# One recurrence with two-set corrections, in-place transposes and a loop in two parts

## The chip, the cores and the metric

The kernel runs on one core of a Trainium2 chip. The metric is the device time of one execution in microseconds (us); smaller is better. TensorE is called PE (its weight loads PEld), VectorE DVE, ScalarE ACT, GpSimd POOL and SyncE SP.

## What is computed

Two residual blocks act on x of 4 x 256 x 32 x 32 floats. The first is a test-time-training layer: after a group norm and a layer norm, 1024 tokens of each image are projected to queries, keys and values of 8 heads of width 32, and a recurrence runs over chunks of 16 tokens. The second is a convolution-like block on a 5 x 5 self-correlation. Only the recurrence is touched:

```
def step(carry, inp):                       # 64 chunks, one after the other
    W1c, b1c = carry
    xq, xk, xv, et = inp
    Z1 = xk @ W1c + b1c
    grad = _ln_l2_bwd(Z1, xv - xk, g, bb)   # gradient of a layer norm's L2 loss
    Attn1 = jnp.tril(xq @ xk.swapaxes(-1, -2))
    b1_bar = b1c - jnp.tril(et) @ grad
    Z1_bar = xq @ W1c - et * Attn1 @ grad + b1_bar
    last_eta = et[..., -1, :, None]
    W1n = W1c - (last_eta * xk).swapaxes(-1, -2) @ grad
    b1n = b1c - (last_eta * grad).sum(-2, keepdims=True)
    return ((W1n, b1n), xq + _ln(Z1_bar, g, bb, EPS_IN))
```

## The kernel before

The recurrence is 64 chunks (`NC`), each for 4 images x 8 heads at once: 128 partitions are 4 pairs of heads x 32 rows (2 heads x 16 tokens), and the free dimension is 4 images x 32. Each engine has an instruction stream written out by hand, and the order between engines comes from counted semaphores, one increment per chunk. ACT, DVE and POOL have all 64 chunks written out; PE writes out chunks 0, 1, 62 and 63 and runs chunks 2 to 61 in a loop of 15 trips of four chunks (`run_chunks`, L1114). A wait whose count depends on the loop variable is computed in registers at the head of a trip.

The trick that shapes the order is that Z of the next chunk is not computed from the updated state. PE forms a *base* for chunk c+1 from the state before the gradient of chunk c is in it (`base`, L1136 to L1160; its last matmul, L1158, adds the bias), and then, when that gradient is known, adds a *correction* to the same PSUM bank (`grads(ZW, ZB[p], o, 1)`, L1167: 16 matmuls of 32x32, which stand as 32 in the trace because every fp32 matmul is two). The correction needs `AM`, the masked key and query products of the chunk.

One chunk c, engine by engine, in program order:

- **PE** (`body`, L1197): waits for the gradient GL of chunk c-1 (`gl`), its masks (`am`) and for the copied products of chunk c (`s1`); correction; `update` of the state with KHX and GL (L1179) and of the bias (L1187); the attention correction of the outputs (L1167 again); a `filler` that computes nothing used (L1194); base of chunk c+1, which waits for the key blocks KT2 from POOL (`kt2`), the query copy (`qr`) and the copied state (`wcopy`); query base (L1231).
- **ACT** (`body`, L1556 on): square of Z after the correction; `out_store` (L1548) of the output rows of chunk c-5; square of output rows (L1538); square root of the variance (L1562) and the variance (L1565), which wait for a DVE sum; `state_w` (L1497), the copy of the updated state that base waits for; `state_b` (L1501); in chunks 40 to 47 a piece of the following stage's scaling (`gain`, L803); `khx` (L1508), `qt2` (L1524), `next_k` (L1517), `products` (L1531, waits for base); square root for the outputs (L1544).
- **DVE** (`body`, L1298 on): sums and the centred Z (L1300 to L1305); target (L1308); reciprocal (L1314); Y (L1319); Y times centred Z (L1322); its two sums (L1323, L1325); two small coefficients (L1328, L1332); YC (L1336), WX (L1338) and GL = WX + YC (L1341); then for older chunks the output variance (`out_var`, L1284), a 32x32 block transpose of output rows (`out_turn`, L1294) and the copy of output rows out of PSUM (`out_rows`, L1279).
- **POOL** (`body`, L1421 on): two small products (L1423, L1426) after DVE's reciprocal; YL (L1428); `blocks` (KT2 of chunk c+2, L1395); `masks` (AM of chunk c+1, L1411, waits for products); `out_norm` of chunk c-3 (L1419, waits for the transpose of chunk c-4, which DVE runs after GL of chunk c); `queries` of chunk c+2 (L1403). In chunk 56 `pre` (L1449) of the following stage comes ahead of `blocks`.

SP only issues DMAs paced by `gl`; none is on the path of a chunk.

## Time and profile before

| what | us |
|---|---|
| median of 3 runs | 583.49 (583.01 to 584.29) |
| the profiled execution | 581.06 |
| its span, first to last instruction | 579.2 |
| first and last `products` of the recurrence start at | 166.8 and 445.9 |
| busy: PE, DVE, ACT, POOL | 483.9, 432.1, 346.2, 327.8 |

All times in the rows are us from the start of the span; durations of single instructions in the lists are in us. A row of the timeline gives the start, the time until the instruction ended, the engine, the source line, operation, operands, how many instructions are merged (x32), and in brackets the idle time before with what ended it. "issue" means that nothing in the profile held the engine back. Instructions of DVE, ACT and POOL overlap a little: the next one starts before the one ahead has written its last result.

### The profile page before, as it was taken

What the parts mean: (1) busy time and instruction counts of PE and PEld (TensorE: products, weight loads), DVE (VectorE), ACT (ScalarE), POOL (GpSimd) and SP (SyncE); (2) the same over time, 40 slices, a digit from 0 to 9 for tenths busy, and PEclk for the clock granted to TensorE, in tenths of its full rate; (3) what the DMA queues carried; (4) which work ended last, traced back from release to release, by engine and by line L of the source; (5) the groups of instructions that cost most, each with busy time, mean ns of one, the idle gap of its engine ahead of it and who ended that gap; (6) DMA issues with size and microseconds to landing.
All of it is one profiled execution on the core that took longest, in us unless ns stands there. A gap on an engine that the chain in (4) does not pass through costs nothing.

```text
span 579.2 us, 30352 instructions
## 1 busy us (share of the span) xinstructions
PE 483.9 (84%) x12556; PEld 313.8 (54%) x12556; DVE 432.1 (75%) x1526; ACT 346.2 (60%) x1166; POOL 327.8 (57%) x590
## 2 busy tenths in 40 slices
PE   0699889898558789888888888888887699998996
PEld 0344334443346577777777676666675244456563
DVE  4757788888746789888888888888885667676652
ACT  2344334322246788888888889988885487553321
POOL 1276888787734466666666655565763667330112
PEclk9999989899858999999999999999997899998998
DMA  8310111111101011111111000011010500000123
GB/s 338 123 24 14 37 37 36 38 36 36 39 9 32 22 37 28 33 32 33 33 28 37 1 1 1 19 36 37 19 37 4 171 1 2 1 2 1 74 75 145
DMA packets 15136, 24.74 MB, mean 43 GB/s; under 512 B 4228, under 2 KB 4968, under 8 KB 15080
## 3 DMA queue, kind: packets, MB, share of 16 engines
q1 hardware_dynamic: 15080, 24.10, 13.8%
q8 instruction: 23, 0.38, 0.3%
q14 instruction: 33, 0.27, 0.2%
HBM read 11.50 MB, written 4.19 MB: 27 GB/s over the span
## 4 chain that ended last, share of the span: by engine, by line
PE 25%; DVE 24%; ACT 12%; issue 8%; POOL 2%; POOLq 0%; ACTq 0%
PE PS L1167 6%; PE PS L924 4%; PE PS L1255 3%; PE PS L906 3%; ACT work L1556 3%; PE PS L361 2%; DVE work L1341 2%; DVE work L1336 2%; DVE work L1322 2%; DVE work L1300 2%; DVE work L1319 2%; DVE PS L1338 2%; DVE PS L1323 2%; DVE PS L1302 2%; DVE PS L1325 2%
## 5 line engine op out<-in xcount | busy, mean ns | idle before, releaser
L1167 PE MATMUL PS<-work 32*32 32x32 f32 x4064 | 59.6, 194 | 37.9 <-DVE work L1341 21.0
L1167 PEld LDWEIGHTS PS<-work 32*32 32x32 f32 x4064 | 53.8, 108 | 43.4 <-issue 43.1
L1411 POOL TENSOR_TENSOR work<-work,mask 128x256 f32<-128x256 f32 x64 | 46.8, 731 | 35.7 <-ACT work L1531 35.7
L512 PE MATMUL PS<-X,work 128*128 128x512 f32 x128 | 63.2, 641 | 0.3 <-ACT X L435 0.3
L1423 POOL TENSOR_TENSOR work<-work,lrh 128x4 f32<-128x4 f32 x64 | 12.9, 201 | 75.6 <-DVE work L1314 70.1
L1300 DVE TENSOR_REDUCE work<-work 128x4 f32<-128x128 f32 x64 | 18.3, 286 | 49.2 <-ACT work L1556 49.2
L663 POOL TENSOR_TENSOR work<-work 128x512 f32<-128x512 f32 x32 | 43.8, 1370 | 7.1 <-DVE work L582 7.1
L1152 PEld LDWEIGHTS PS<-work 64*32 64x32 f32 x2048 | 32.9, 110 | 24.9 <-issue 23.6
L1152 PE MATMUL PS<-work 64*32 64x64 f32 x2048 | 43.6, 225 | 2.9 <-issue 2.0
L1194 PE MATMUL PS<-cst 128*128 128x256 f32 x126 | 45.1, 440 | 0.0
L1179 PE MATMUL PS<-work 32*64 32x32 f32 x2016 | 43.0, 222 | 2.2 <-issue 2.2
L1508 ACT ACTIVATE work<-TK,small 128x128 f32<-128x128 f32 x128 | 44.3, 402 | 0.0
L1524 ACT ACTIVATE work<-QP,cst 128x128 f32<-128x128 f32 x128 | 43.9, 396 | 0.0
L1395 POOL TENSOR_TENSOR work<-KP,cst 128x256 f32<-128x256 f32 x64 | 39.2, 612 | 6.5 <-POOLq L454 6.5
L512 PEld LDWEIGHTS PS<-X,work 128*128 128x128 f32 x128 | 25.3, 206 | 29.5 <-issue 28.7
L881 POOL TENSOR_TENSOR TK<-TK 128x512 f32<-128x512 f32 x7 | 9.0, 1304 | 53.5 <-ACT TK L1077 53.5
L1179 PEld LDWEIGHTS PS<-work 32*64 32x64 f32 x2016 | 35.8, 135 | 3.9 <-issue 1.3
L581 DVE TENSOR_TENSOR work<-PS,work 128x512 f32<-128x512 f32 x32 | 21.8, 683 | 21.4 <-POOL KP L666 19.1
L1544 ACT ACTIVATE work<-work,small 128x4 f32<-128x4 f32 x64 | 19.0, 296 | 24.7 <-DVE work L1284 24.6
L377 ACT ACTIVATE work<-X 128x512 f32<-128x512 f32 (+1 forms) x16 | 9.7, 630 | 40.0 <-DVE X L368 40.0
L1255 PE MATMUL PS<-TK,wsm 128*128 128x512 f32 x64 | 31.4, 616 | 1.5 <-ACT X L1600 1.5
L1158 PE MATMUL PS<-work,cst 128*128 128x128 f32 x128 | 32.2, 334 | 0.0
(162 smaller groups left out, 1344.5 us busy)
## 6 DMA issues: line engine op xcount, KB each, us to landing
X<-in_x SPq DMA_DIRECT2D x4, 1024.0 KB, 8.2
TK<-KP SPq DMA_DIRECT2D x64, 64.0 KB, 1.9
X<-QP SPq DMA_DIRECT2D x64, 64.0 KB, 2.0
TK<-in_x SPq DMA_DIRECT2D x16, 256.0 KB, 3.0
out<-TK SPq DMA_DIRECT2D x16, 256.0 KB, 2.4
work<-in_rope SPq DMA_DIRECT2D x2, 512.0 KB, 9.1
cst<-in_consts SPq DMA_DIRECT2D x1, 289.0 KB, 5.0
work<-in_wk SPq DMA_DIRECT2D x1, 256.0 KB, 11.2
```

The lines of the kernel that those rows point to most:

```text
L512: mm = nc.tensor.matmul(PS[:, 2 + m, :], lhs(j), xt(i, j), start=(j == 0), stop=(j == J - 1))
L663: nc.gpsimd.tensor_tensor(ksw[:, t, :], ksw[:, t, :], sinT[:, h], ALU.mult).then_inc(s_ksin, 1)
L1152: mm = nc.tensor.matmul(PS[HD * a:HD * a + HD, ZB[p], b * ZW:b * ZW + ZW], KT2[p][r:r + 64, k * B + b, :, :].rearrange("p e t -> p (e t)") ...
L1158: nc.tensor.matmul(PS[:, ZB[p], 0:B * ZW].rearrange("p (b n) -> p b n", b=B)[:, :, 0:HD], ident, Bs[1 - p if past(n, 1) else 0], start=Fal ...
L1167: mm = nc.tensor.matmul(PS[HD * a:HD * a + HD, bank, b * width:b * width + HD], AM[p][HD * a:HD * a + HD, b, part, :, :].rearrange("p e t ...
L1179: mm = nc.tensor.matmul(PS[2 * HD * a2:2 * HD * a2 + 2 * HD, WB + k, b * HD:b * HD + HD], KHX[p][HD * a:HD * a + HD, b, :, :].rearrange("p ...
L1194: nc.tensor.matmul(PS[:, QB[p], 256:512], ident, ccol("spread", 0, 256), start=True, stop=True, skip_group_check=True)
L1255: mm = nc.tensor.matmul(PS[:, 2 + m, :], wsm[:, j, m * P:(m + 1) * P], ot(i, j), start=(j == 0), stop=(j == J - 1))
L1395: nc.gpsimd.tensor_tensor(KT2[p], chunk(KP, c).unsqueeze(2).broadcast_to([P, J * B, E, CS]), ccol("emask_k").unsqueeze(1).unsqueeze(3).bro ...
L1411: nc.gpsimd.tensor_tensor(AM[p].rearrange("p b s e t -> p (b s) e t"), S1[p].unsqueeze(2).broadcast_to([P, 2 * B, E, CS]), mask2.rearrange ...
L1508: kx = nc.scalar.activation(KHX[p][:, :, e, :].rearrange("p b (f t) -> p b f t", f=E), head_rows(1, c), ACT.Copy, scale=upd_mask[:, e:e + 1])
L1524: a = nc.scalar.activation(QT2[p][:, :, e, :], chunk(QP, c), ACT.Copy, scale=ccol("emask_k", e, 1))
```

## The change

PE adds the correction in two sets: one from YC as soon as that exists, one from WX, and the second releases ACT; GL is awaited afterwards, for the update. The filler stays in chunks 1 to 13 and is gone after; the PE loop becomes two loops, of 3 trips with filler and 12 without, and the query base becomes a function. DVE reorders its sums and coefficients, runs `out_var` ahead of GL, and transposes output rows straight into `TT`, so ACT's `out_store` and the buffer ZT go. ACT runs `products` before `qt2`. POOL runs `out_norm` and `queries` first, then waits for GL of its own chunk, then `masks` and `blocks`. WX moves from PSUM to SBUF.

```diff
-        TS, SQ, YL, YC = (carve(B, HD) for _ in range(4))
+        TS, SQ, YL, YC, WX = (carve(B, HD) for _ in range(5))
         YY = carve(2, B, HD)
...
             def run_chunks(eng, body):
                 for c in range(2):
-                    body(c, c % 2)
-                with nc.Fori(0, NC // 4 - 1, engines=(mybir.EngineType.PE,), hint_back_edge=True) as four:
-                    for k in range(4):
-                        body(four * 4 + (2 + k), k % 2)
+                    body(c, c % 2, fill=True)
+                for first, trips, fill in ((2, FILLED, True), (2 + 4 * FILLED, NC // 4 - 1 - FILLED, False)):
+                    with nc.Fori(0, trips, engines=(mybir.EngineType.PE,), hint_back_edge=True) as four:
+                        for k in range(4):
+                            body(four * 4 + (first + k), k % 2, fill=fill)
                 for c in range(NC - 2, NC):
                     body(c, c % 2)
+            FILLED = 3
...
-                def grads(width, bank, p, part):
+                def grads(width, bank, p, part, rows):
...
-                def body(c, p):
-                    o = 1 - p
-                    done, now, nxt = value(pe, c), value(pe, c + 1), value(pe, c + 2)
-                    before = value(pe, c - 1) if past(c, 2) else None
-                    if past(c, 1):
-                        pe.wait_ge(q["init"], 1)
-                        pe.wait_ge(q["gl"], done)
-                        pe.wait_ge(q["am"], done)
-                        pe.wait_ge(q["s1"], now)
-                        grads(ZW, ZB[p], o, 1).then_inc(q["corr"], 1)
-                        pe.wait_ge(q["init"], 1)
-                        pe.wait_ge(q["khx"], done)
-                        pe.wait_ge(q["bcopy"], done)
-                        update(o)
-                        grads(HD, QB[o], o, 0).then_inc(q["attn"], 1)
-                        if past(c, 2):
-                            pe.wait_ge(q["zq"], before)
-                        filler(p)
-                    else:
-                        base(0, 0, 1, 1)
-                    if not is_last(c):
-                        base(c + 1, o, nxt, now)
-                    else:
-                        pe_mean(pe, 0, True)
+                def query_base(ready, p, drained):
                     pe.wait_ge(q["init"], 1)
-                    pe.wait_ge(q["qt2"], now)
-                    pe.wait_ge(q["wcopy"], now)
-                    if past(c, 2):
-                        pe.wait_ge(q["zq"], before)
+                    pe.wait_ge(q["qt2"], ready)
+                    pe.wait_ge(q["wcopy"], ready)
+                    if drained is not None:
+                        pe.wait_ge(q["zq"], drained)
...
                     mm.then_inc(q["qbase"], 1)
+                def body(c, p, fill=False):
+                    o = 1 - p
+                    done, now, nxt = value(pe, c), value(pe, c + 1), value(pe, c + 2)
+                    before = value(pe, c - 1) if past(c, 2) else None
+                    if past(c, 1):
+                        pe.wait_ge(q["init"], 1)
+                        pe.wait_ge(q["yc"], done)
+                        pe.wait_ge(q["am"], done)
+                        pe.wait_ge(q["s1"], now)
+                        grads(ZW, ZB[p], o, 1, YC)
+                        pe.wait_ge(q["init"], 1)
+                        pe.wait_ge(q["w"], done)
+                        grads(ZW, ZB[p], o, 1, WX).then_inc(q["corr"], 1)
+                        pe.wait_ge(q["init"], 1)
+                        pe.wait_ge(q["gl"], done)
+                        pe.wait_ge(q["khx"], done)
+                        pe.wait_ge(q["bcopy"], done)
+                        update(o)
+                        grads(HD, QB[o], o, 0, GL[o]).then_inc(q["attn"], 1)
+                        if fill:
+                            if before is not None:
+                                pe.wait_ge(q["zq"], before)
+                            filler(p)
+                    else:
+                        base(0, 0, 1, 1)
+                    if not is_last(c):
+                        base(c + 1, o, nxt, now)
+                    else:
+                        pe_mean(pe, 0, True)
+                    query_base(now, p, before)
...
                     dve.wait_ge(q["zn"], c + 1)
-                    nc.vector.transpose(ZT.rearrange("p b d -> p (b d)"), ZN.rearrange("p b d -> p (b d)")
-                                        ).then_inc(q["zt"], 1)
+                    nc.vector.transpose(
+                        TT.rearrange("p e (b n) -> p b e n", b=B)[:, :, :, c * CS:(c + 1) * CS],
+                        ZN.rearrange("p b (e t) -> p b e t", e=E)).then_inc(q["ot"], 1)
...
                     nc.vector.tensor_tensor(YY[:, 0, :, :], PZ, TS, ALU.add).then_inc(q["y"], 1)
                     dve.wait_ge(q["y"], c + 1)
                     dve.wait_ge(q["zc"], c + 1)
+                    nc.vector.tensor_reduce(sums[:, 0:B], YY[:, 0, :, :], AX.X, ALU.add).then_inc(q["my"], 1)
                     nc.vector.tensor_tensor(YY[:, 1, :, :], YY[:, 0, :, :], ZC, ALU.mult).then_inc(q["yp"], 1)
-                    nc.vector.tensor_reduce(sums[:, 0:B], YY[:, 0, :, :], AX.X, ALU.add).then_inc(q["my"], 1)
-                    dve.wait_ge(q["yp"], c + 1)
-                    nc.vector.tensor_reduce(sums[:, B:2 * B], YY[:, 1, :, :], AX.X, ALU.add).then_inc(q["m"], 1)
                     dve.wait_ge(q["u"], c + 1)
                     dve.wait_ge(q["my"], c + 1)
                     nc.vector.scalar_tensor_tensor(cc0, sums[:, 0:B], -1.0 / HD, lead[:, 0, :],
                                                    ALU.mult, ALU.mult).then_inc(q["cy"], 1)
+                    dve.wait_ge(q["yp"], c + 1)
+                    nc.vector.tensor_reduce(sums[:, B:2 * B], YY[:, 1, :, :], AX.X, ALU.add).then_inc(q["m"], 1)
+                    dve.wait_ge(q["yl"], c + 1)
+                    dve.wait_ge(q["cy"], c + 1)
+                    nc.vector.tensor_tensor(YC, YL, bc(cc0), ALU.add).then_inc(q["yc"], 1)
                     dve.wait_ge(q["m"], c + 1)
                     dve.wait_ge(q["u2"], c + 1)
                     nc.vector.scalar_tensor_tensor(cc1, sums[:, B:2 * B], -1.0 / HD, lead[:, 1, :],
                                                    ALU.mult, ALU.mult).then_inc(q["c"], 1)
-                    dve.wait_ge(q["yl"], c + 1)
-                    dve.wait_ge(q["cy"], c + 1)
-                    nc.vector.tensor_tensor(YC, YL, bc(cc0), ALU.add).then_inc(q["yc"], 1)
                     dve.wait_ge(q["c"], c + 1)
                     nc.vector.tensor_tensor(WX, ZC, bc(cc1), ALU.mult).then_inc(q["w"], 1)
-                    dve.wait_ge(q["w"], c + 1)
                     dve.wait_ge(q["yc"], c + 1)
-                    nc.vector.tensor_tensor(GL[p], WX, YC, ALU.add).then_inc(q["gl"], 1)
                     if past(c, 2):
                         out_var(c - 2)
+                    dve.wait_ge(q["w"], c + 1)
+                    nc.vector.tensor_tensor(GL[p], WX, YC, ALU.add).then_inc(q["gl"], 1)
...
                     if past(c, 1):
-                        pool.wait_ge(q["zt"], c + 0)
+                        pool.wait_ge(q["ot"], c + 0)
                     nc.gpsimd.tensor_tensor(ZN, ZQ[c % 3], bc(sdq[1 - p]), ALU.mult).then_inc(q["zn"], 1)
...
-                    if not near_end(c):
-                        blocks(c + 2, p)
-                    if not is_last(c):
-                        masks(c + 1, 1 - p)
                     if past(c, 3):
                         out_norm(c - 3, 1 - p)
                     if not near_end(c):
                         queries(c + 2, p)
+                    pool.wait_ge(q["gl"], c + 1)
+                    if not is_last(c):
+                        masks(c + 1, 1 - p)
+                    if not near_end(c):
+                        blocks(c + 2, p)
...
-                def out_store(c):
-                    act.wait_ge(q["zt"], c + 1)
-                    nc.scalar.activation(
-                        TT.rearrange("p e (b n) -> p e b n", b=B)[:, :, :, ds(c * CS, CS)],
-                        ZT.rearrange("p b (e t) -> p e b t", e=E), ACT.Copy).then_inc(q["ot"], 1)
...
-                    if not is_last(c):
-                        qt2(c + 1, 1 - p)
                     if not isinstance(c, int) or c + 3 < NC:
                         next_k(c + 2, p)
                     if not is_last(c):
                         products(c + 1, 1 - p)
+                        qt2(c + 1, 1 - p)
```

## Rows read from the trace of the kernel before

**Rows 1.** Busy times by stretch: start and end, length, busy us and instructions, PEclk, DMA.

```profile
178.00:198.00 20.00, 15.59 (x688) 12.12 (x688) 14.21 (x70) 13.84 (x57) 9.63 (x27) 1.00 0.10 23
...
248.20:264.90 16.70, 14.82 (x688) 11.82 (x688) 14.65 (x73) 14.05 (x60) 10.57 (x29) 1.00 0.13 32
```

**Rows 2.** Timeline of ACT in one chunk.

```profile
303.61 0.28 ACT L1556 ACTIVATE work<-PS 128x128 f32<-128x128 f32 x1
...
304.63 0.42 ACT L1497 ACTIVATE work<-PS 128x128 f32<-128x128 f32 x2
...
306.47 0.36 ACT L1531 ACTIVATE work<-PS,small 128x128 f32<-128x128 f32 x1
...
307.68 0.28 ACT L1556 ACTIVATE work<-PS 128x128 f32<-128x128 f32 x1
```

**Rows 3.** Timeline of DVE in the same chunk.

```profile
305.03 0.29 DVE L1319 TENSOR_TENSOR work<-PS,work 128x128 f32<-128x128 f32 x1
305.36 0.29 DVE L1322 TENSOR_TENSOR work<-work,PS 128x128 f32<-128x128 f32 x1
...
306.76 0.29 DVE L1341 TENSOR_TENSOR work<-PS,work 128x128 f32<-128x128 f32 x1
307.01 0.29 DVE L1284 TENSOR_REDUCE work<-work 128x4 f32<-128x128 f32 x1
307.21 0.30 DVE L1294 STREAM_TRANSPOSE work<-work 128x128 f32<-128x128 f32 x1
```

**Rows 4.** Timeline of PE in the same chunk.

```profile
304.71 0.70 PE L1194 MATMUL PS<-cst 128*128 128x256 f32 x2
305.34 0.65 PE L1152 MATMUL PS<-work 64*32 64x64 f32 x32
...
307.16 0.45 PE L1167 MATMUL PS<-work 32*32 32x32 f32 x32 [0.36 <-DVE work L1341]
307.54 0.67 PE L1179 MATMUL PS<-work 32*64 32x32 f32 x32
```

**Rows 5.** Timeline of the one chunk in which POOL is late (57).

```profile
416.33 0.62 POOL L1395 TENSOR_TENSOR work<-KP,cst 128x256 f32<-128x256 f32 x1
...
416.90 0.78 POOL L1411 TENSOR_TENSOR work<-work,mask 128x256 f32<-128x256 f32 x1
...
417.64 0.39 POOL L1419 TENSOR_TENSOR work<-work 128x128 f32<-128x128 f32 x1
...
417.99 0.28 POOL L1403 COPY work<-QP 128x128 f32<-128x128 f32 x1
...
418.45 0.52 PEld L1152 LDWEIGHTS PS<-work 64*32 64x32 f32 x32 [1.49 <-issue]
```

**Rows 6.** Timeline of ACT in a chunk with a piece of the scaling.

```profile
348.44 0.69 ACT L1524 ACTIVATE work<-QP,cst 128x128 f32<-128x128 f32 x2
349.02 0.30 ACT L1517 ACTIVATE work<-KP 128x128 f32<-128x128 f32 x1
```

**Rows 7.** Timeline of PE in the loop's first trip, one of its stalls.

```profile
183.86 0.67 PE L1179 MATMUL PS<-work 32*64 32x32 f32 x32 [1.18 <-issue]
```

**Rows 8.** DMA queues that fetch instructions, from 172 to 198.

```profile
q8 instruction: 6, 0.10, 1.5%
```

**Rows 9.** DMA queues from 198.5 to 437, all that moved anything.

```profile
q1 hardware_dynamic: 3891, 5.84, 9.4%
q14 instruction: 24, 0.20, 0.3%
```

**Rows 10.** Timeline of PE after the loop ends, chunk 62.

```profile
440.55 0.44 PE L1167 MATMUL PS<-work 32*32 32x32 f32 x17 [3.11 <-issue]
440.93 1.08 PE L1179 MATMUL PS<-work 32*64 32x32 f32 x32
...
446.83 0.67 PE L1179 MATMUL PS<-work 32*64 32x32 f32 x32
```

**Rows 11.** Busy times by stretch, as rows 1, in that chunk.

```profile
441.00:443.00 2.00, 2.00 (x73) 1.83 (x73) 1.59 (x8) 1.80 (x9) 0.28 (x2) 0.50 0.03 8
```

More of the change, by code:

```diff
@@ L760, in build @@
         ZQ = [carve(B, HD) for _ in range(3)]
-        SQQ, ZN, ZT = (carve(B, HD) for _ in range(3))
+        SQQ, ZN = (carve(B, HD) for _ in range(2))
         ss, sz, ssq, sd1 = (carve(B) for _ in range(4))
@@ L776, in home @@
             return PS[:, 7, at * B * HD:(at + 1) * B * HD].rearrange("p (b d) -> p b d", b=B)
-        PZ, WX, ZC = (home(at) for at in range(3))
-        at = 3 * B * HD
+        PZ, ZC = (home(at) for at in range(2))
+        at = 2 * B * HD
         cc0, sums = PS[:, 7, at:at + B], PS[:, 7, at + B:at + 3 * B]
@@ L1098, in build @@
             names = ("init my cy updw wcopy bcopy kt2 qt2 qr kr khx base qbase corr s1 am p sq ss sz zc v sd r ts y yp m u u2 "
-                     "yl c w yc gl upd attn zq sqq ssq sdq rq zn zt ot").split()
+                     "yl c w yc gl upd attn zq sqq ssq sdq rq zn ot").split()
             q = {n: sem(f"scan_{n}") for n in names}
@@ L1169, in grads @@
                                                       "p e t -> p (e t)"),
-                                                  GL[p][HD * a:HD * a + HD, b, :],
+                                                  rows[HD * a:HD * a + HD, b, :],
                                                   start=False, stop=True, skip_group_check=True)
@@ L1233, in body @@
                                     QT2[p][r:r + 64, k * B + b, :, :].rearrange("p e t -> p (e t)"),
-                                    R[o][r:r + 64, k, b, 0:HD], start=(b == 0), stop=False,
+                                    R[1 - p][r:r + 64, k, b, 0:HD], start=(b == 0), stop=False,
                                     skip_group_check=True)
                     mm.then_inc(q["qbase"], 1)
+                def body(c, p, fill=False):
[28 more added lines that the diff above has]
+                    query_base(now, p, before)
                 run_chunks(pe, body)
@@ L1240, in _ @@
                 pe.wait_ge(q["am"], NC)
-                grads(HD, QB[1], 1, 0).then_inc(q["attn"], 1)
+                grads(HD, QB[1], 1, 0, GL[1]).then_inc(q["attn"], 1)
                 def project(i, first):
@@ L1354, in _ @@
                 out_var(NC - 2)
-                dve.wait_ge(q["ot"], NC - 4)
                 out_turn(NC - 4)
@@ L1361, in _ @@
                 out_r(NC - 1)
-                dve.wait_ge(q["ot"], NC - 3)
                 out_turn(NC - 3)
@@ L1365, in _ @@
                 dve_scale(dve, 0)
-                dve.wait_ge(q["ot"], NC - 2)
                 out_turn(NC - 2)
-                dve.wait_ge(q["ot"], NC - 1)
                 out_turn(NC - 1)
@@ L1556, in body @@
                     nc.scalar.activation(SQ, zb, ACT.Square).then_inc(q["sq"], 1)
-                    if past(c, 5):
-                        out_store(c - 5)
                     if past(c, 2):
@@ L1615, in _ @@
                 out_square(NC - 2, 0)
-                out_store(NC - 5)
                 out_sd(NC - 2, 0)
-                out_store(NC - 4)
                 out_square(NC - 1, 1)
@@ L1622, in _ @@
                 out_sd(NC - 1, 1)
-                out_store(NC - 3)
                 act_square(act, 1, False)
                 act_affine(act, 0)
-                out_store(NC - 2)
-                out_store(NC - 1)
                 act.wait_ge(q["ot"], NC)
```

## Prediction

> **What bounds the kernel now.** I looked first for the stretch that repeats. Of the recurrence's 64 chunks, 60 are 15 trips of one PE loop, so a change in a chunk counts sixty-fold. The busy times by stretch show the loop's first trip, 688 matmuls in 20.0 us, and a later trip, the same 688 in 16.70 us at a granted clock of 1.00, the upper of its two levels (2.4 GHz) [rows 1]. No engine is full: in those 16.70 us PE is busy for 14.82, DVE 14.65, ACT 14.05, POOL 10.57. A chain through all of them sets the time. The timeline of one chunk shows it: ACT's square at 303.61 begins the chunk, the next square comes at 307.68, so a chunk is 4.07 [rows 2]; four make 16.28, and the head of a trip, where waits are computed in registers, adds the other 0.42. I count from the square. DVE's sums run on to GL, which starts at 3.15 and ends at 3.44 [rows 3]; PE's correction starts 0.11 later, at 3.55, and the next square 0.52 after that [rows 4, 2]. So the chain today is square, DVE, GL, correction, and GL's 0.33 is what the change goes for. Second comes a chain that nearly keeps up: the state copy ends at 1.44, the filler holds base until 1.73, products start at 2.86 and end at 3.22 [rows 2, 4]. The correction needs the products too, and here they wait 0.3 for GL.
>
> **DVE's new order.** A step that needs the one ahead starts 0.33 after it, one that does not 0.20 [rows 3]. From Y at 1.42: its sum at 1.75, the product at 1.95, the small coefficient at 2.15, the second sum at 2.28, YC at 2.47 (YL permitting), the other coefficient at 2.67, WX at 2.87, the old output variance at 3.07, GL at 3.27. WX ends at 3.16, so the input of the last correction is 0.28 sooner than GL was, and GL itself is 0.12 later. WX in SBUF instead of PSUM I cost at nothing: GL writes SBUF today in the same 0.29.
>
> **PE's two sets.** A set of 32 takes 0.38 to issue [rows 4]. The first set also has the waits on the products in front of it, though it is released by YC. This is the first thing that turns against the change: products must now be there 0.38 earlier. Without filler, base can start at 1.44 + 0.11 (that step from one engine to PE was seen above). Base to products is 1.13 [rows 4, 2] (there ACT came free at the same moment, so it is an upper end), products take 0.36, then 0.11 to PE, 0.38 for the first set and 0.52 from the second set to the square. The chunk is 1.55 + 2.50 = 4.05, the same as today. The removed output store on ACT does not shorten it, since it stood where ACT waits for DVE's first sum; moving `qt2` behind the products only takes it out of a place where it now ends just in time. With the filler (0.63 [rows 4]) base starts at 1.73 and the chunk is 4.23.
>
> **POOL's new order.** The output normalisation waits for a transpose that DVE runs after GL. Before, nothing urgent stood behind it; now `queries`, `masks` and `blocks` do, and PE's base waits for `blocks`. After GL at 3.27 the transpose starts 0.25 later and takes 0.30 [rows 3], 0.11 to POOL (as above, an estimate), then one after the other 0.35, 0.28, 0.74 and 0.62, read from the one chunk in which POOL ran without a pause; there PE's base started 0.18 after POOL's last needed instruction [rows 5]. KT2 of chunk c+2 is thus usable 3.27 + 0.25 + 0.30 + 0.11 + 1.99 + 0.18 = 6.10 after the square of chunk c, and the square of chunk c+2 comes 2.50 after that. Two chunks take 8.60, one 4.30. This is above both 4.05 and 4.23, so I take it for filled and unfilled chunks alike. POOL is then free again at 5.92 - 4.30 = 1.62, about when DVE's reciprocal, the step ahead of Y at 1.42, lets it start the next chunk, so YL is late by a tenth at most. The masks have a chunk to spare. A trip is 2 x 8.60 + 0.42 = 17.62 against 16.70, 0.92 more. If POOL's spans flatter me and it is off the path, a trip is 4 x 4.05 + 0.42 = 16.62 (-0.1); if the transpose takes twice its 0.30 because it writes runs of 16, a chunk is 4.45 and a trip 18.2 (+1.5). I take 0.92 because each link is a row of the same instructions.
>
> **What that adds up to.** Trips at the steady rate: the second and third of the first loop, and of the second loop's twelve all but the first and the two with the pieces of scaling: 11 x 0.92 = +10.1 (bounds -1.1 and +16.5). In the eight chunks with scaling ACT's products end the wait; `qt2` ahead of them took 0.58 [rows 6], the earlier need takes 0.38 back, 8 x 0.20 = -1.6, of which I count -1.2 because the heads of two trips are no longer hidden there.
>
> **Code loading.** The first trip took 20.0 for the matmuls of a 16.7 trip: PE stops for issue, once for 1.18 [rows 7], and q8, a queue that carries instructions, moves six packets then and none in the later trips, while q14 goes on throughout [rows 8, 9]. That is 29.1 ns for each matmul with its weight load [rows 1]. A trip grows from 688 matmuls to 816 with filler and 808 without. First loop, first trip: 816 x 29.1 = 23.7, +3.7 on the 20.0 of before. Second loop, first trip: 23.5 where the old loop ran on in 16.7, +6.8. The lower bound of that is the old first trip, +3.3; the upper adds the stall of 3.11 with which PE left its loop [rows 10], +9.9. Chunks 62 and 63 I leave as they are: one set more and no filler.
>
> Sum: 10.1 - 1.2 + 3.7 + 6.8 = +19.4 on the profiled execution's 581.06, so 600.5. The median of the runs is 2.4 above that execution; 603 is the forecast for the median.
>
> **Rivals.** *The first loop does not stay loaded.* Today q8 is silent between 198.5 and 437 [rows 9], so 688 matmuls with their loads stay. 816 is a fifth more. If they do not, its two later trips cost 23.7 instead of 17.62, +12: 615. The Trainium skill (Runtime: NRT & Kernel Launch, Instruction fetch mechanics) gives PE room for 2048 instructions, by which an estimated 1670 (two for each matmul, and the waits) would fit. It also says that a taken branch to outside a window of two blocks fetches anew. For the loop of before the trace agrees with the first and not with the second [rows 9]. This rival has 8%.
>
> *The clock stays down.* After the 3.11 stall PE ran at 0.50, the lower level (1.2 GHz), and the chunk from one update to the next took 5.90 [rows 10, 11] before the clock came back, with filler in it. The change from loop to loop brings such a stall, and behind it is no filler. PE's own 3.71 a chunk (14.82 over four) becomes 3.46; scaled by 5.90/3.71 it is 5.5, 1.2 over 4.30, for 44 chunks +53: 656. Against it: the stalls of the first trip, up to 1.18 [rows 7], left the clock at 1.00 [rows 1]. The Trainium skill (TensorE: Matmul & The Clock Gate, Part 1) has the slow level as the default and activity as what lifts it, a rule that speaks against taking filler away; no row here shows a recovery without filler. This rival has 8%.
>
> *The gradient chain alone sets the chunk*, the other side. If products end by 2.78 and `blocks` a quarter of a microsecond sooner than I say, the chunk is WX's 3.16 + 0.11 + 0.52 = 3.79, a trip 15.58, 11 x -1.12 = -12.3; with -1.2 and the code's +10.5 that is -3.0, 580.5. It decides at the wait for the products: base would have to start 0.3 ahead of the state copy that it waits for. I give it 5%.
>
> *A draw* needs POOL off the path and the second loop's code nearly free: -1.1 - 1.2 + 3.7 and next to nothing for its entry. I give it 3%.
>
> **How the numbers follow.** The main case has 76%. Its own bounds go from 603 - 10.1 - 1.1 - 3.5 = 588 (POOL off the path, cheap entry) to 603 + 6.4 + 3.1 = 612; the first rival at 615 with a little more for a slower transpose makes 618. Outside are the clock (8%), the other side (5%), a draw (3%) and the tails. Within 0.2% (1.2 us, about what a measurement of this kernel can tell from no change) I call the same. Slower has everything but the last two rivals: 92%.
>
> **What would show it.** Right: the first set waits for ACT's products, not for DVE's YC; the normalisation on POOL starts just after DVE's transpose, and base waits for `blocks`, not for ACT; squares 4.2 to 4.4 apart with and without filler; a first trip of 23 to 24 us in both loops, with instruction packets at the second one's start. Wrong: squares 3.8 apart, or the second loop entered without a stall; or a PE clock of 0.50 beyond the second loop's first trip.

## The result and the profile after

The changed kernel takes 620.71 us (median of 4 runs, 618.82 to 624.09) against 583.89 (583.01 to 586.09): ratio 1.0631, 95% interval 1.0576 to 1.0686. The profiled execution took 620.45, its span is 618.6 us and its mean granted clock 0.873; before, 581.06, 579.2 and 0.959. Ratios here leave disturbed runs out while medians take in every run, so that for one kernel below, the one without filler, the two don't match.

The page of the changed kernel, costliest groups (last part: idle time ahead of the group and what ended it), answers first who waits for whom.

```profile
L1170 PE MATMUL PS<-work 32*32 32x32 f32 x6080 | 88.8, 207 | 26.6 <-ACT work L1541 14.2
...
L1427 POOL TENSOR_TENSOR work<-work 128x128 f32<-128x128 f32 x64 | 25.6, 400 | 92.9 <-DVE TK L1305 89.8
L1155 PE MATMUL PS<-work 64*32 64x64 f32 x2048 | 51.3, 250 | 23.1 <-POOL work L1403 16.5
```

The same two PE groups in the kernel before:

```profile
L1167 PE MATMUL PS<-work 32*32 32x32 f32 x4064 | 59.6, 194 | 37.9 <-DVE work L1341 21.0 <-ACT work L1531 7.7 <-POOL work L1411 5.9
L1152 PE MATMUL PS<-work 64*32 64x64 f32 x2048 | 43.6, 225 | 2.9 <-issue 2.0 <-ACT work L1497 1.0
```

PE's correction sets (L1170) now wait for ACT's products (L1541), and for DVE in two places only (2.4 us, was 21.0). Of the 14.2 us put down to the products, 8.6 stand at the heads of 11 trips, where the products had ended 0.5 to 0.8 earlier and the time is the head's own work in registers (experiment 6); the other 5.7, in 30 places, are a wait for them. POOL's output normalisation (L1427) waits 89.8 us for DVE's transpose, and base (L1155) waits 16.5 for POOL's blocks (L1403). One chunk of the first loop, in which PE still has its filler, shows the same links in a timeline (start, us, engine and line).

```profile
213.55 0.28 ACT L1560 ACTIVATE work<-PS 128x128 f32<-128x128 f32 x1 [0.17 <-PE PS L1170]
...
214.52 0.61 POOL L1403 TENSOR_TENSOR work<-KP,cst 128x256 f32<-128x256 f32 x1
...
214.65 0.63 DVE L1320 TENSOR_TENSOR work<-TK,work 128x128 f32<-128x128 f32 x1
...
215.34 0.65 PE L1155 MATMUL PS<-work 64*32 64x64 f32 x32
...
216.36 0.28 DVE L1344 TENSOR_TENSOR work<-work,PS 128x128 f32<-128x128 f32 x1
...
216.45 0.37 ACT L1541 ACTIVATE work<-PS,small 128x128 f32<-128x128 f32 x1 [0.51 <-PE PS L1161]
...
216.74 0.29 DVE L1350 TENSOR_TENSOR work<-PS,work 128x128 f32<-128x128 f32 x1
...
216.96 0.74 PE L1170 MATMUL PS<-work 32*32 32x32 f32 x64 [0.17 <-ACT work L1541]
217.15 0.28 DVE L1355 TENSOR_TENSOR work<-work 128x128 f32<-128x128 f32 x1
...
217.34 0.30 DVE L1305 STREAM_TRANSPOSE TK<-work 128x128 f32<-128x128 f32 x1
...
217.73 0.40 POOL L1427 TENSOR_TENSOR work<-work 128x128 f32<-128x128 f32 x1 [1.42 <-DVE TK L1305]
217.75 0.28 ACT L1560 ACTIVATE work<-PS 128x128 f32<-128x128 f32 x1 [0.17 <-PE PS L1170]
...
218.85 0.35 DVE L1320 TENSOR_TENSOR work<-TK,work 128x128 f32<-128x128 f32 x1
...
219.01 0.66 POOL L1403 TENSOR_TENSOR work<-KP,cst 128x256 f32<-128x256 f32 x1
...
219.77 0.65 PE L1155 MATMUL PS<-work 64*32 64x64 f32 x32 [0.17 <-POOL work L1403]
```

The square comes at 213.55 and again at 217.75, 4.20 later. YC (L1344) is done at 216.64, the products (L1541) at 216.82, and both sets (64 matmuls) start at 216.96: the first set's early input buys nothing. WX (L1350), the second set's input, is done at 217.03, before that set's turn: a set takes 0.38 to issue [rows 4]. POOL's normalisation starts 0.09 after the transpose ends, and 2.04 later base starts.

The windows (length; busy us and instructions of PE, PEld, DVE, ACT, POOL; granted clock; DMA) tell the rest. They are the first loop's first trip and, roughly, its third; the second loop's first; a later one; and a stretch of low clock.

```profile
178.40:203.00 24.60, 20.70 (x820) 16.54 (x824) 13.82 (x70) 13.54 (x56) 10.30 (x27) 0.78 0.11 26
...
222.80:240.50 17.70, 16.36 (x824) 13.24 (x825) 14.89 (x72) 13.44 (x56) 10.46 (x29) 1.00 0.12 30
...
240.50:267.50 27.00, 21.63 (x816) 18.12 (x816) 14.21 (x72) 13.96 (x57) 11.94 (x30) 0.61 0.12 29
...
278.00:295.40 17.40, 13.85 (x814) 11.93 (x812) 14.41 (x72) 13.50 (x57) 9.81 (x28) 1.00 0.11 28
...
359.99:376.10 16.11, 16.11 (x611) 13.97 (x614) 10.66 (x54) 11.19 (x43) 8.24 (x23) 0.50 0.00 1
```

A trip at the upper clock is 17.70 with filler, where it was 16.70 [rows 1]. Without filler the window shown has 17.40, but it begins two chunks behind a low stretch; the one trip whose four chunks (30 to 33) all ran at the upper clock took 17.73. In the second loop the clock doesn't stay up. From 359.99 on, PE is busy all of 16.11 us and does only three chunks' matmuls, at 0.50, the lower level (1.2 GHz). A chunk that is low from end to end takes 5.37 to 5.40. The matmuls around the place where it fell are these:

```profile
338.98 0.65 PE L1155 MATMUL PS<-work 64*32 64x64 f32 x32 [0.90 <-POOL work L1403]
341.26 0.74 PE L1170 MATMUL PS<-work 32*32 32x32 f32 x64 [0.82 <-ACT work L1541]
...
355.28 0.47 PE L1170 MATMUL PS<-work 32*32 32x32 f32 x32
356.64 0.65 PE L1155 MATMUL PS<-work 64*32 64x64 f32 x32 [0.90 <-POOL work L1403]
...
358.86 1.08 PE L1170 MATMUL PS<-work 32*32 32x32 f32 x64 [0.77 <-ACT work L1541]
359.87 1.08 PE L1182 MATMUL PS<-work 32*64 32x32 f32 x32
```

Behind two ordinary waits at the head of a trip, 0.90 and 0.77, the 32 update matmuls take 1.08 instead of 0.67. There is no long stall, and one trip earlier the like waits, 0.90 and 0.82, were followed by no fall. Later the clock comes back by itself and falls again. Of chunks 18 to 61, 13 ran low in whole or in part (leaving out a tenth of chunk 25, and chunk 61, in which PE leaves the loop).

Where the time went, from square to square (us):

| chunks | before | after | difference | forecast |
|---|---|---|---|---|
| 0 to 2, with the start of 0 | 178.69 | 178.36 | -0.3 | 0 |
| 2 to 6, first loop's first trip | 20.58 | 24.67 | +4.1 | +3.7 |
| 6 to 14, its other trips | 33.47 | 37.51 | +4.0 | +1.8 |
| 14 to 18, second loop's first trip | 16.67 | 26.94 | +10.3 | +6.8 |
| 18 to 41 and 49 to 62, the rest of that loop | 155.50 | 174.45 | +18.9 | +8.3 |
| 41 to 49, scaling but for its first chunk | 36.16 | 35.12 | -1.0 | -1.2 |
| 62, 63 and all after it | 138.15 | 141.60 | +3.5 | 0 |

The differences add up to the +39.4 between the two profiled executions. Scaling lengthens chunks 40 to 47; chunk 40, which ran low, stands in the row above. The 13 low chunks took 71.2 us; the same 13 at the length of their neighbours at the upper clock would be an estimated 57.9. So about 13.3 of the 18.9 in chunks 18 to 41 and 49 to 62 is the clock, and 5.6 is what else is longer.

### The profile page after: what moved, and what is told of

It reads as the page before. It is cut to its first block, busy times and chain, and to the rows that moved or that the text cites. A ratio compares the mean times of both kernels' runs of the same rounds, so it can differ in the third digit from the quotient of the medians.

```text
span 618.6 us, 34244 instructions
## 1 busy us (share of the span) xinstructions
PE 514.3 (83%) x14472; PEld 351.3 (57%) x14472; DVE 430.0 (70%) x1526; ACT 338.6 (55%) x1102; POOL 330.1 (53%) x590
## 3 DMA queue, kind: packets, MB, share of 16 engines
HBM read 11.50 MB, written 4.19 MB: 25 GB/s over the span
## 4 chain that ended last, share of the span: by engine, by line
PE 42%; issue 11%; POOL 8%; ACT 6%; DVE 6%; POOLq 0%; ACTq 0%; DVEq 0%
PE PS L1170 9%; PE PS L1155 6%; PE PS L1161 4%; PE PS L1182 4%; PE PS L924 3%; PE PS L1266 3%; PE PS L361 3%; PE PS L906 3%; PE PS L1190 2%; PE PS L1210 2%; POOL work L1419 2%; POOL work L1403 2%; ACT work L1541 2%; PE PS L946 1%; PE PS L1197 1%
## 5 line engine op out<-in xcount | busy, mean ns | idle before, releaser
L1170 PE MATMUL PS<-work 32*32 32x32 f32 x6080 | 88.8, 207 | 26.6 <-ACT work L1541 14.2
L1170 PEld LDWEIGHTS PS<-work 32*32 32x32 f32 x6080 | 82.9, 120 | 33.2 <-issue 31.2
L1427 POOL TENSOR_TENSOR work<-work 128x128 f32<-128x128 f32 x64 | 25.6, 400 | 92.9 <-DVE TK L1305 89.8
L1155 PE MATMUL PS<-work 64*32 64x64 f32 x2048 | 51.3, 250 | 23.1 <-POOL work L1403 16.5
L1155 PEld LDWEIGHTS PS<-work 64*32 64x32 f32 x2048 | 40.1, 126 | 32.9 <-issue 30.8
L1182 PE MATMUL PS<-work 32*64 32x32 f32 x2016 | 49.9, 239 | 2.5 <-issue 2.3
L1541 ACT ACTIVATE work<-PS,small 128x128 f32<-128x128 f32 x64 | 23.5, 367 | 51.7 <-PE PS L1161 51.7
L1182 PEld LDWEIGHTS PS<-work 32*64 32x64 f32 x2016 | 43.3, 155 | 6.6 <-issue 2.8
L1403 POOL TENSOR_TENSOR work<-KP,cst 128x256 f32<-128x256 f32 x64 | 40.8, 637 | 5.3 <-POOLq L454 5.3
L1560 ACT ACTIVATE work<-PS 128x128 f32<-128x128 f32 x64 | 17.8, 278 | 33.3 <-PE PS L1170 32.6
L1210 PE MATMUL PS<-work 64*32 64x32 f32 x2048 | 33.5, 210 | 0.0
```

Of the source, the lines that this page charges most:

```text
L1155: mm = nc.tensor.matmul(PS[HD * a:HD * a + HD, ZB[p], b * ZW:b * ZW + ZW], KT2[p][r:r + 64, k * B + b, :, :].rearrange("p e t -> p (e t)") ...
L1170: mm = nc.tensor.matmul(PS[HD * a:HD * a + HD, bank, b * width:b * width + HD], AM[p][HD * a:HD * a + HD, b, part, :, :].rearrange("p e t ...
L1182: mm = nc.tensor.matmul(PS[2 * HD * a2:2 * HD * a2 + 2 * HD, WB + k, b * HD:b * HD + HD], KHX[p][HD * a:HD * a + HD, b, :, :].rearrange("p ...
L1210: mm = nc.tensor.matmul(PS[HD * a:HD * a + HD, QB[p], b * HD:b * HD + HD], QT2[p][r:r + 64, k * B + b, :, :].rearrange("p e t -> p (e t)") ...
L1403: nc.gpsimd.tensor_tensor(KT2[p], chunk(KP, c).unsqueeze(2).broadcast_to([P, J * B, E, CS]), ccol("emask_k").unsqueeze(1).unsqueeze(3).bro ...
L1541: nc.scalar.activation(S1[p].rearrange("p (b s) t -> p b (s t)", b=B), PS[:, ZB[p], 0:B * ZW].rearrange("p (b n) -> p b n", b=B)[:, :, HD:ZW],
```

## The experiments

The first theory: taking the filler out of the second loop lets the clock fall, entering a second loop costs its code, and the longer trip comes from products and POOL. The rival is that chunks are long because of the order of the work alone, and the clock only follows.

**1. One loop, all filled.** The changed kernel with a single loop of 15 trips, so that neither a second loop nor an unfilled chunk up to 61 is left.

```diff
-for first, trips, fill in ((2, FILLED, True), (2 + 4 * FILLED, NC // 4 - 1 - FILLED, False)):
+for first, trips, fill in ((2, NC // 4 - 1, True),):
```

> The changed kernel with one loop of 15 trips, filler in every chunk. If taking the filler away is what lets the clock fall: granted clock 1.00 from chunk 2 to 61, trips of about 17.5 us as in chunks 6 to 13 of the changed kernel, no code fetched in mid-loop, 597 to 601 us in all (13 trips at +0.8, first trip +4, before it +2, the scaling chunks -1). If the clock falls for another reason (more waiting in a chunk): clock well below 1.00 in the loop, 610 or more.

Measured: 599.76 (595.63 to 601.97), ratio 1.0259 (1.0188 to 1.0331), mean clock 0.943. Windows inside the loop:

```profile
215.00:300.00 85.00, 77.59 (x3940) 62.96 (x3940) 72.25 (x345) 64.61 (x269) 50.40 (x134) 1.00 0.12 30
300.00:400.00 100.00, 91.56 (x4599) 74.09 (x4589) 85.80 (x408) 81.49 (x327) 60.54 (x161) 1.00 0.06 16
```

The clock is 1.00 throughout, as it is in these windows of the kernel before, and none of chunks 7 to 61 is low. Trips are 17.63 to 17.85. What is left over the kernel before, 2.6%, is the order of the work, with the first trip's larger code (its chunks take 25.3, 4.7 more) and a low chunk 6, which has its filler.

**2. One loop, unfilled.**

```diff
-for first, trips, fill in ((2, FILLED, True), (2 + 4 * FILLED, NC // 4 - 1 - FILLED, False)):
+for first, trips, fill in ((2, NC // 4 - 1, False),):
```

> The changed kernel with one loop and no filler in it. If the filler holds the clock: the clock falls and comes back time after time through the whole recurrence, chunks of 5.4 beside chunks of 4.0 to 4.4, 612 to 625 us, so no better than the change although it pays for no second loop. If the second loop is to blame: clock 1.00 and chunks near 4.2 to 4.3, 597 or less.

Measured: 607.63 (601.43 to 607.96), ratio 1.0363 (1.029 to 1.0436), clock 0.888.

```profile
215.00:300.00 85.00, 70.06 (x3710) 60.71 (x3710) 68.16 (x334) 63.03 (x260) 49.98 (x131) 0.90 0.12 30
300.00:400.00 100.00, 82.12 (x4444) 71.15 (x4443) 80.93 (x394) 79.71 (x316) 58.23 (x152) 0.91 0.06 16
```

The same windows now average 0.90 and 0.91: whole stretches of two to four chunks (17 to 20, 41 to 44, 53 to 55, 57 and 58) at 5.37 where they are low throughout, then the upper level again. A trip that is wholly at the upper level takes 17.59 to 17.67. So the clock falls in an unfilled loop that has no second loop's entry ahead of it, as expected, but recovers sooner than I had thought; the total is below what was expected.

**3. Two loops, both filled.** Only the second loop, its entry and its exit, differs from experiment 1.

```diff
-for first, trips, fill in ((2, FILLED, True), (2 + 4 * FILLED, NC // 4 - 1 - FILLED, False)):
+for first, trips, fill in ((2, FILLED, True), (2 + 4 * FILLED, NC // 4 - 1 - FILLED, True)):
```

> The changed kernel with its two loops of 3 and 12 trips, filler in both. It differs from the run with one loop by the second loop's entry alone: if that costs what the code's loading costs, 7 to 9 us more than with one loop, a dip of the clock of a few us at the entry, and the clock back at 1.00 afterwards: 604 to 610. If it is the entry's stall that brings the clock down for good, and not the missing filler: close to the change's 620.

Measured: 613.72 (611.62 to 614.27), ratio 1.0504 (1.0441 to 1.0567). That is 14 over experiment 1, where 7 to 9 was expected. PE's stalls at the second loop's entry and at the last exit:

```profile
244.60 0.41 PE L1190 MATMUL PS<-work,ones_blk 32*32 32x128 f32 x1 [1.93 <-issue]
...
264.36 0.38 PE L1170 MATMUL PS<-work 32*32 32x32 f32 x20 [1.62 <-issue]
...
468.19 0.64 PE L1170 MATMUL PS<-work 32*32 32x32 f32 x29 [3.40 <-issue]
```

Its chunks 14 to 18 take 27.79, 10.0 more than the 17.77 of experiment 1, and the end from chunk 49 on another 4.6 more, nearly all of it from chunk 61 on, in which PE leaves the loop. In the window of the entry the clock is 0.77, and from 270 on it is 1.00 and stays there, which it doesn't in the changed kernel, whose second loop has no filler:

```profile
240.00:270.00 30.00, 23.82 (x933) 18.51 (x919) 15.46 (x79) 15.16 (x62) 12.62 (x32) 0.77 0.11 26
270.00:400.00 130.00, 119.14 (x5982) 96.30 (x5979) 111.80 (x531) 103.95 (x420) 77.21 (x205) 1.00 0.07 19
```

These three and the changed kernel make a square: 599.8 and 607.6 with one loop, filled and not; 613.7 and 620.7 with two. The second loop costs 14 and 13, taking the filler out 8 and 7. By the ratios it is 14 and 16, 6 and 7, with 5 to 6 either way, so the filler's share in the whole time is barely clear of the spread of the runs; the traces show it chunk by chunk. Both effects are there whatever the other does, which is more than the rival allows.

**4. Two sets alone.** The kernel before, with the two correction sets, DVE's order and WX in SBUF, and nothing else (PE's part of the edit is shown).

```diff
-pe.wait_ge(q["gl"], done)
+pe.wait_ge(q["yc"], done)
...
-grads(ZW, ZB[p], o, 1).then_inc(q["corr"], 1)
+grads(ZW, ZB[p], o, 1, YC)
+pe.wait_ge(q["w"], done)
+grads(ZW, ZB[p], o, 1, WX).then_inc(q["corr"], 1)
```

> The kernel before with the two sets of corrections and DVE's new order alone (filler, POOL's and ACT's orders, the copy on ACT as before). If the products bound the first set: chunks of 4.2 to 4.25 instead of 4.07, with scaling 4.95 instead of 4.58, a first trip 4 longer, 597 to 602 us. If the sets bring forward what they are meant to: chunks of 3.8, 578 or less.

Measured: 599.64 (598.54 to 600.02), ratio 1.0275 (1.0251 to 1.0299). PE's correction sets by line:

```profile
L1167 PE MATMUL PS<-work 32*32 32x32 f32 x6080 | 80.0, 196 | 27.9 <-ACT work L1535 23.7 <-issue 3.4 <-POOL work L1415 0.9
```

23.7 of their 27.9 us of waiting is put down to ACT's products, none to DVE; 8.5 of it stands at the heads of 11 trips, where the products had long ended, and 15.1, in 47 places, is a wait for them. A chunk is 4.19 to 4.22 where it was 4.07, a scaling chunk 4.86 where it was 4.58, and the first trip 25.57. The chunk is what the prediction's sum for filled products gives (4.23). The part that was meant to shorten the chain lengthens it, by itself. With the filler in, the clock still fell once behind the first trips, for chunks 57 and 58, after waits of 0.98 and 0.77; the kernel before had 1.11 and 0.82 there and no fall.

**5. POOL's order alone**, in the kernel before.

```diff
-blocks(c + 2, p); masks(c + 1, 1 - p); out_norm(c - 3, 1 - p); queries(c + 2, p)
+out_norm(c - 3, 1 - p); queries(c + 2, p)
+pool.wait_ge(q["gl"], c + 1)
+masks(c + 1, 1 - p); blocks(c + 2, p)
```

> The kernel before with POOL's new order alone. If base waits for the blocks behind the transpose: two chunks take 8.3 to 8.5 (GL at 3.15, 3.03 on to usable blocks, 2.12 on to the square), trips 17.0 to 17.4, 588 to 594 us. If the order is free, as it looks from masks that have a chunk to spare: 583 to 586.

Measured: 587.66 (587.2 to 595.79), ratio 1.012 (1.0043 to 1.0197). Base now waits for the blocks here too, 6.9 us where it was none:

```profile
L1152 PE MATMUL PS<-work 64*32 64x64 f32 x2048 | 44.0, 225 | 9.0 <-POOL work L1395 6.9 <-issue 1.1 <-ACT work L1499 1.0
L1395 POOL TENSOR_TENSOR work<-KP,cst 128x256 f32<-128x256 f32 x64 | 42.7, 667 | 5.4 <-POOLq L454 5.4
```

A trip is 17.00 against 16.67, the low end of what was expected. POOL's chain is on the path, but not by the whole 0.92 a trip.

**6. All filled, POOL's old order** (experiment 1 with the order of before).

```diff
-out_norm(c - 3, 1 - p); queries(c + 2, p)
-pool.wait_ge(q["gl"], c + 1)
-masks(c + 1, 1 - p); blocks(c + 2, p)
+blocks(c + 2, p); masks(c + 1, 1 - p); out_norm(c - 3, 1 - p); queries(c + 2, p)
```

> The run with one filled loop, with POOL's order of before (blocks and masks ahead of the output normalisation). If POOL's new order is what makes base wait: base waits for the filler and the state copy again, every chunk about 4.2 (1.73 to base and 2.50 on to the square), trips 17.2 instead of 17.7, 593 to 595 us. If POOL is beside the path: trips stay at 17.7 and the time at 599.

Measured: 596.9 (596.19 to 598.84), ratio 1.0245 (1.0218 to 1.0273). Trips are 17.42, three chunks at 4.19 and one at 4.84: 0.3 less than in experiment 1, and by the ratios alone not told apart from it. The trip is longer than expected because the head of a trip now costs 0.65, not 0.42:

```profile
309.13 0.37 ACT L1539 ACTIVATE work<-PS,small 128x128 f32<-128x128 f32 x1 [0.51 <-PE PS L1161]
...
310.29 0.74 PE L1170 MATMUL PS<-work 32*32 32x32 f32 x64 [0.81 <-ACT work L1539]
```

These sets, at a trip's head, come 0.81 after PE's last matmul. The bracket names the products, but those ended at 309.50, 0.79 before. What is left for it is the head's own work, registers and the jump back, which the profile does not count as busy. In other chunks the sets wait 0.17. In the kernel before PE stood idle for about as long at a head (0.77 and 0.83), but 0.36 of it was the wait for GL that every chunk had, so only 0.42 showed.

**7. Half the filler**, one loop, POOL's old order (experiment 6 with 128 columns in place of 256).

```diff
-nc.tensor.matmul(PS[:, QB[p], 256:512], ident, ccol("spread", 0, 256), start=True, stop=True,
+nc.tensor.matmul(PS[:, QB[p], 256:384], ident, ccol("spread", 0, 128), start=True, stop=True,
```

> The changed kernel in one loop with POOL's order of before and half the filler (128 columns) in every chunk. The half, 0.32, fits into the 0.44 in which PE waits for the state copy, so a chunk should be the unfilled 4.0 at a clock of 1.00 if half is enough to hold it: trips 16.4, 583 to 586 us. If the clock needs the whole: falls and recoveries as in the unfilled loop, chunks of 5.4 among them, 595 or more.

Measured: 596.29 (596.09 to 596.95), ratio 1.0226 (1.0204 to 1.0249), clock 0.911.

```profile
178.00:198.00 20.00, 19.22 (x645) 16.30 (x644) 10.26 (x52) 10.71 (x43) 7.25 (x19) 0.50 0.08 20
...
215.00:300.00 85.00, 76.82 (x4091) 65.51 (x4080) 75.64 (x363) 67.43 (x282) 54.41 (x142) 1.00 0.13 32
300.00:400.00 100.00, 89.35 (x4742) 76.06 (x4730) 86.51 (x421) 82.72 (x333) 62.83 (x163) 1.00 0.06 18
```

Once up, the clock stays up from 215 to 400 and a trip is 16.97 to 17.06, 0.4 shorter. But the first trip and chunk 6 ran at 0.50 throughout, and three more chunks (57 to 59) took 6.1 to 6.5, which gives all of it back. A miss: the total is some 10 above what was expected.

**8. The kernel before without its filler.** The filler matmuls, which compute nothing that is used, are left out, with the wait ahead of them.

```diff
-if past(c, 2):
-    pe.wait_ge(q["zq"], before)
-filler(p)
```

> The kernel before without its filler, nothing else changed. If the filler holds the clock by itself: falls and recoveries in the loop, chunks of 5 and more among chunks of 4.07, 595 or more. If the clock falls in the changed kernel because of its longer waits in a chunk: the clock stays at 1.00 here and the time at 582 to 585, since GL's chain sets the chunk with or without filler.

Measured: ratio 1.0248 (1.0199 to 1.0297); runs from 595.92 to 624.03; clock 0.837 in the profile.

```profile
300.00:320.00 20.00, 18.76 (x685) 16.00 (x685) 15.67 (x78) 14.87 (x62) 11.02 (x29) 0.58 0.11 27
320.00:340.00 20.00, 14.93 (x824) 12.85 (x827) 16.33 (x81) 16.31 (x71) 12.04 (x32) 0.99 0.03 7
340.00:360.00 20.00, 16.54 (x714) 14.07 (x713) 16.38 (x82) 17.17 (x67) 11.83 (x32) 0.78 0.00 1
```

At the upper level a chunk is 4.06, the same as with filler: the filler takes no time on the path of the kernel before. But 27 of the 56 chunks 6 to 61 ran low in part or whole, the ordinary ones at up to 4.95. In the kernel before with filler, none of chunks 6 to 60 is low. This settles the filler apart from everything else in the change: taking it out lets the clock swing in the old order too. A low chunk with two sets is 0.42 dearer (5.37), about one set more at that clock.

**9. The transposes and the products, each alone and together**, in the kernel before. The second edit also takes out ACT's `out_store` and the waits for it (not shown).

```diff
-    if not is_last(c):
-        qt2(c + 1, 1 - p)
...
         products(c + 1, 1 - p)
+        qt2(c + 1, 1 - p)
```

```diff
-nc.vector.transpose(ZT.rearrange("p b d -> p (b d)"), ZN.rearrange("p b d -> p (b d)")
-                    ).then_inc(q["zt"], 1)
+nc.vector.transpose(TT.rearrange("p e (b n) -> p b e n", b=B)[:, :, :, c * CS:(c + 1) * CS],
+                    ZN.rearrange("p b (e t) -> p b e t", e=E)).then_inc(q["ot"], 1)
```

> The kernel before with the in-place transposes alone. The copy that goes from ACT stood ahead of a wait for DVE's first sum, so nothing in ordinary chunks; in the eight with scaling ACT's own work ends the wait, and there too the sum comes after the copy: 583 to 584, the same as before. If ACT's total is what counts: 0.2 less in each of the eight, 581 to 582.

> The kernel before with products ahead of the query blocks alone. In the eight chunks with scaling products come 0.58 sooner and GL ends the wait instead: 4.07 instead of 4.58, 579 to 581, all of what the two parts together brought. If the copy on ACT has its share: 582 to 583.

> The kernel before with only two parts of the change: transposes that write the output rows in place (no copy on ACT) and products ahead of the query blocks. If GL's chain sets the ordinary chunks and ACT's products only those with scaling: ordinary chunks stay at 4.07, the eight with scaling go from 4.58 to 4.07, 579 to 581 us. If the slower POOL wait for the transpose or the transpose's pattern costs something: chunks above 4.07, 584 or more.

Measured: transposes alone 584.68 (583.62 to 587.64), ratio 1.0037 (0.9999 to 1.0075); products alone 581.37 (579.91 to 589.3), 0.9964 (0.9925 to 1.0003); both 580.18 (577.47 to 586.57, 12 runs), 0.9935 (0.9893 to 0.9977). The last beats both kernels. ACT in a scaling chunk of that version:

```profile
345.12 0.36 ACT L1528 ACTIVATE work<-PS,small 128x128 f32<-128x128 f32 x1
345.37 0.69 ACT L1521 ACTIVATE work<-QP,cst 128x128 f32<-128x128 f32 x2
...
346.20 0.28 ACT L1547 ACTIVATE work<-PS 128x128 f32<-128x128 f32 x1
```

The products (L1528) end at 345.48, ahead of `qt2` (L1521), and a scaling chunk is 4.07, as any other, where it was 4.58. From square 41 to 49 it is 33.60 instead of 36.16, and 33.66 with the products alone; with the transposes alone it stays at 36.16. So the 2.5 us (3.1 with chunk 40) are the products', though the whole-run interval of the products alone just reaches 1. That the transposes add anything is not shown: alone they give 1.0037, which also reaches 1. In the trace with the transposes alone, filler in, the clock fell for chunks 57 and 58, as in experiment 4.

## Why the prediction was right and wrong

**Right: the direction, and what binds the chunk.** The products came to bind the first set and POOL's blocks came to bind base, both by name [rows 4, 5]. The removed 0.33 of GL bought nothing, as the sum of base, products and one set said (experiment 4, 4.19 against 4.23). A trip at the upper clock is 17.59 to 17.67 without filler (experiment 2) and 17.63 to 17.85 with it (experiment 1), forecast 17.62. Each link was near its row: base to products 1.11 (1.13), products to the sets 0.51 (0.47 with the step to PE), transpose to normalisation 0.09 (0.11). That the trip comes so close is in part luck: the head of a trip costs 0.65, where the sum had the 0.42 of before, and the pairs of chunks are a little under 8.60. The longer trip comes from both causes, too: filled, experiment 6 gives 17.42 by the products and the trip's head, and POOL's order adds 0.3.

**Right: the first trip, the scaling, the first loop's code.** The first trip cost +4.1 for +3.7, though its clock was 0.78, which the 29.1 ns a matmul [rows 1] did not contain. Scaling gave -1.0 for -1.2 (seven of its eight chunks), and experiment 9 shows the move that earned it. The first loop stays loaded: its third trip takes 17.70, and q8, which brought the code of both first trips, moves nothing between 203 and 240, the first loop's later trips, nor between 261 and 473, nearly the whole second loop, which is as large (DMA queues of the second of these stretches, all that moved anything):

```profile
q1 hardware_dynamic: 2784, 4.33, 7.5%
q14 instruction: 17, 0.14, 0.2%
```

So the rival in which the larger loop doesn't stay loaded was wrong. The Trainium skill (Runtime: NRT & Kernel Launch, Instruction fetch mechanics) gives PE room for 2048 instructions, which the trace agrees with, and has a taken branch beyond two blocks fetch anew, which it again does not show.

**Wrong: the clock, which the sum left at nothing.** The forecast was 603, in a range up to 618; it came to 620.7. The step that failed is the one that took the second loop's chunks as "2 x 8.60" at the upper clock, with a clock that stays down as a rival at 8%. Its argument, that "the stalls of the first trip, up to 1.18 [rows 7], left the clock at 1.00 [rows 1]", looked at a stretch with filler in it, and the rival asked only whether the clock comes back after one stall. What happens is neither: it comes back without filler, and falls again at ordinary waits, so that 13 of 44 chunks ran low, not all or none. That is the prediction's own sign of being wrong, a clock of 0.50 beyond the second loop's first trip. The price was right (5.37 against 5.5 a chunk). It is some 13.3 us in chunks 18 to 61, and about 2 more in chunk 6, which took 6.29 at the low clock (the rest of +4.0 there is the two longer trips); chunk 6 has its filler, and took 6.38 and 6.40 in the filled kernels of experiments 1 and 3, so that part is not for want of it. Against the filled second loop of experiment 3, which takes 163.8 for the chunks that take 174.5 here, the missing filler costs 10.6 (the two profiled executions differ by 8.8 in all). Experiments 1, 2 and 8 show the cause: filler in, the clock nearly always up; filler out, the clock swings, in the old order and in the new. Filler is no guarantee, by chunks 57 and 58 in experiments 4 and 9, and what sets off a single fall is open: like waits are followed by a fall or by none. The Trainium skill (TensorE: Matmul & The Clock Gate, A second HAM failure mode: psum-queue depth-cycling) tells of a kernel in which short idle spells between groups of matmuls made the clock swing between its levels; the trace agrees, with pauses of 0.90 and 0.77 ahead of a fall.

**Mis-sized: the second loop's entry, and its exit.** The mechanism, code that has to be fetched, was right: six packets on q8 between 240.5 and 260.6, and PE stalls:

```profile
243.05 0.42 PE L1190 MATMUL PS<-work,ones_blk 32*32 32x128 f32 x1 [1.65 <-issue]
...
485.06 0.42 PE L1182 MATMUL PS<-work 32*64 32x32 f32 x4 [1.55 <-issue]
```

The term "Second loop, first trip: 23.5" measured 26.94, +10.3 for +6.8, just beyond its upper bound of +9.9. The clock is 0.61 in that window, but a filled second loop pays as much (27.79, experiment 3), so it is not for want of filler. What lies behind chunk 62 was taken as 0 and is +3.5: the second stall above falls in chunk 63's update. Why it stands there and not in the kernel before is open, but the end goes with the second loop: from square 61 on, the exit from the loop included, the two kernels with two loops take 149.0 each and the eleven with one 144.4 to 147.5.

**Sum.** Of the 20 us between +19.4 and +39.4, 13.3 are the clock in the second loop, 2 the clock in chunk 6, 3.5 the entry and 3.5 the end; against these, what is left of the nine steady trips of the second loop came at +5.6 where +8.3 was forecast. Told by whole runs, the miss of 17.7 (603 to 620.7) has the same parts: one filled loop, 599.8, is 3.6 above the forecast less its 6.8 for the entry; the second loop, 14, is 7 above that 6.8; and taking the filler out costs the last 7.

**Not tried.** The wait for the copied products (`s1`) stands ahead of both sets. Putting it behind the first set would have PE write a PSUM bank that ACT still reads, so no kernel here does it.

## What to carry to other kernels

Before a wait is split, see in the timeline which other wait ends just ahead of it: here the products were there only 0.2 before GL (3.22 and 3.44 after the square), and half a step taken out of one chain only pulled the other onto the path, with one set more to pay. Matmuls that compute nothing may take no time and still keep the clock up; before they go, measure the kernel without them, alone. An order in which urgent work stands behind a wait for something unhurried (POOL's normalisation ahead of blocks) is a new chain, and a second copy of a large loop was paid here at its entry and at its end. When a bracket names what ended a wait, check that it ended then: at the head of a trip the products had ended 0.79 earlier.

## What the runs showed of the hardware that was not expected

The granted clock falls and rises again many times in a loop that never stops for long: in the kernel before without filler it was 0.58, 0.99 and 0.78 in three neighbouring windows of 20 us. With half the filler's columns it was at 1.00 for 185 us once it was there, but 0.50 from 178 to 198, in the first trip, where it was 0.75 with the whole filler (experiment 6).

DVE and POOL hold each other up. DVE's L1320, which reads two SBUF tensors, took 0.63 at 214.65 while POOL's blocks ran from 214.52 to 215.13, and 0.35 at 218.85, when POOL's came after it; with POOL's old order (experiment 6) it took 0.29 on average. The blocks were slowed in their turn, from a mean of 612 ns in experiment 6 to 667 in experiment 5, where POOL's order alone was changed. In the chunk shown GL starts 3.60 after the square, and 3.27 was the sum; the 0.33 between is the 0.34 that L1320 took longer than the 0.29 of other chunks. The Trainium skill (SBUF — State Buffer, SBUF: two separate sides) has the two engines take turns on a shared pair of ports when DVE reads two tensors from SBUF; the trace agrees. How much of a trip it costs was not measured by itself.
